# Mamba loop: state on 128 partitions, chosen rows scaled between exponentials, residual update behind masked B and C

## The chip, the cores and the metric

One core of a Trainium2 chip runs the program. The metric is the device time of one execution in microseconds; the median of three runs is compared. The profile comes from one execution of its own.

## What is computed

x is (4, 1024, 256). Three layers run in turn, each behind a plain layer norm: a mixture of 8 experts (top 2, squared ReLU, times 0.5), a Mamba block, and the same mixture again. The Mamba block matters here:

```python
xn = (x - mu) * rsqrt(var + EPS) * ln_w + ln_b
u = xn @ W_in                       # z (512), xBC (544), dt (64)
dt = softplus(u[..., -NHEADS:] + dt_bias)
xBC = silu(causal_conv4(xBC) + conv_b)
xs, Bm, Cm = xBC split in 64 heads x 8, 16, 16
A = -exp(A_log)
def step(h, inp):                   # over 1024 steps, h is (4, 64, 8, 16)
    h = h * exp(dt_t * A) + dt_t x_t B_t
    y = h C_t
g = (y + Dp * xs) * silu(z)
g = g * rsqrt(mean(g * g) + EPS) * rms_w
return x + g @ W_out
```

The outer sum then adds the layer's normed input once more, so the update of x is x + (normed x) + g @ W_out.

## The kernel before

Three stages run one after the other: routing and experts (0 to about 330 us), the Mamba loop (about 376 to 985), routing and experts again. In the Mamba stage 32 chunks k are worked on. A chunk is 32 time steps of all 4 sequences, 128 tokens on 128 partitions. The recurrence is cut up by chunk: inside a chunk the heads' outputs are matrix products with decay factors (`decays`, `intra`); between chunks a state `Hs` is carried.

`Hs` lies on 64 partitions (4 sequences x 16 state entries) and has 512 columns (64 heads x 8). The 0/1 mask `C_HALF` leaves in `bm` and `cm` (64 x 128) for each token only the 16 rows of its own sequence. For chunk k the state takes this way:

- TensorE `sums`, L1199: running sums of dt*A in `banks[0]`, three groups of 64 columns: up to the token, past the token, whole chunk. ScalarE `sums`, L1062, exponentiates all 192 columns into `ee`.
- TensorE `inter`, L1204: `cm` times `Hs` into `banks[7]` (128 x 512). VectorE `carried`, L890, multiplies it by `ee` into `yi`.
- VectorE `weighted`, L896, makes `dtxw`; `skipped`, L903, adds the D term to `yi`; `faded`, L908, multiplies `Hs` by the chunk's decay.
- TensorE `state`, L1224: B transposed (`bt`) times `dtxw` into `banks[7][0:64]`, once `carried` has read the bank; VectorE `state`, L914, adds it to `Hs`.

The other names that count: L920 `decays` (four products of decay factors and B.C pairs, from ScalarE's exponentials L1068 of TensorE's L1217), L856 `conv` (15 operations), L884 `gate_in`, L862 `silu` (needs ScalarE's tanh `tanh_conv`, L1109), L868 and L869 `masked`, L834 to L844 `steps` (dt and dt*A by a chain of small operations), L874 `pairs`, L879 `stepped` (`dtx`), L933 `finish` (the update of x with the row factor `mss` that GpSimd makes in `rms`, L985 and L989, from the sum of squares of ScalarE's `squares`, L1073).

The two rows of expert output that were chosen for each token are loaded by SyncE (`load`), scaled by ScalarE (`choices`, L1056, two operations) and added to x by GpSimd's accumulating DMAs (`add_choice`, L1000, the first of a chunk one round before it is normed).

Nothing schedules this: each engine has one function with a loop over i that calls these steps for chunks i-1 to i+5 in a written order, and it works through them strictly in that order, waiting on semaphores. `after(engine, name, count)` is such a wait, for a buffer to come free. On VectorE a round is `carried`, `weighted`, `skipped`, `faded`, `stats`, `decays` 0, `gate`, `state`, `decays` 1, `norm`, `decays` 2 and 3, `conv`, `finish`, `gate_in`, `silu`, `masked`, `steps`, `pairs`, `stepped`. On ScalarE the round ends with `channels`, `turned_b` (L1146, which waits for VectorE's `pairs`) and `choices`.

Of the kernel before, what the change touches and what calls it, by code (L numbers as in the profile page):

```python
# [14 lines left out]
P = 128  # L15
# [66 lines left out]
def build(nc, a, out):  # L82
    with ExitStack() as ctx:
# [6 lines left out]
        banks = [ctx.enter_context(nc.psum_tensor(f"bank{i}", [P, 512], F32)) for i in range(8)]  # L90
# [106 lines left out]
        cm = [sb(f"cm{p}", [B * DS_, P]) for p in range(2)]  # L197
# [11 lines left out]
        ee = sb("ee", [P, 3 * NH])  # L209
        Hs = sb("Hs", [B * DS_, DI])  # L210
# [577 lines left out]
        sums_ps = banks[0][:, 2 * P + NH:2 * P + 4 * NH]  # L788
# [6 lines left out]
        def mamba_dve(dve):  # L795
# [69 lines left out]
            def masked(k):  # L865
                n = B * DS_
                dve.wait_ge(S("m_si"), k + 1)
                dve.tensor_tensor(bm[:, :], th[0:n, NB * P:], const(C_HALF)[0:n, :], ALU.mult).then_inc(S("m_g"), 1)  # L868
                dve.tensor_tensor(cm[k % 2][:, :], th[n:2 * n, NB * P:], const(C_HALF)[n:2 * n, :], ALU.mult)\  # L869
                    .then_inc(S("m_g"), 1)  # L870
# [65 lines left out]
            for i in range(FIRST, LAST):  # L936
# [110 lines left out]
        def mamba_act(act):  # L1047
# [94 lines left out]

            def turned_b(k):
                act.wait_ge(S("m_cbp"), k + 1)
                act.wait_ge(S("m_cb"), k + 1)
                act.activation(bt[k % 2][:, :], bt_ps, ACT.Copy).then_inc(S("m_bt"), 1)  # L1146

            for i in range(FIRST, LAST):
                if inside(i):
                    sums(i)  # L1150
                    decays(i, 0)
                    decays(i, 1)
                    decays(i, 2)
                    decays(i, 3)
# [17 lines left out]
                if inside(i + 1):  # L1172
                    turned_b(i + 1)
                if inside(i + 4):
                    choices(i + 4)

        def mamba_pe(pe):
# [13 lines left out]
            def sums(k):  # L1191
# [5 lines left out]
                for i, mask in enumerate((upto16, past16, chunk16)):  # L1197
# [22 lines left out]
            def state(k):  # L1220
# [3 lines left out]
                pe.matmul(banks[7][0:B * DS_, :], bt[k % 2][:, :], dtxw[:, :], start=True, stop=True).then_inc(S("m_sp"), 1)  # L1224
# [70 lines left out]
            def pairs(k):  # L1295
# [6 lines left out]
                for b in range(B):  # L1302
                    pe.matmul(cb_ps, bm[:, :], cm[k % 2][:, b * QT:(b + 1) * QT], start=b == 0, stop=b == B - 1)
# [149 lines left out]
```

## Time and profile before

| | us |
|---|---|
| three runs | 1360.13, 1356.54, 1357.54, median 1357.54 |
| profiled execution, time | 1360.11 |
| its span in the trace | 1358.3 |
| Mamba loop, 376.0 to 985.5 | 609.5 |
| VectorE busy in it | 537.8 |
| TensorE busy in it | 525.1 |
| ScalarE busy in it | 327.9 |
| GpSimd busy in it | 279.4 |

The span leaves out 1.8 us that the execution's time has. Busy time of VectorE and ScalarE counts operations alone, which overlap a little at their ends, so 128x512 elements take 0.68 us but the next operation starts 0.60 behind. Spans on GpSimd are rough.

### The profile page before, as it was taken

Reading aid. Unit: us, or ns where it says so; the run is one execution under the profiler, and the core shown is the slowest. Engines: PE = TensorE matmul, PEld = TensorE weight load, DVE = VectorE, ACT = ScalarE, POOL = GpSimd, SP = SyncE. Lnnn points to the kernel's source line nnn. Section 1 sums busy time; section 2 is a strip of 40 time slices with the busy share of each in tenths; the row PEclk is TensorE's granted clock in tenths of the full one; section 3 lists DMA queues with packets and bytes.
Section 4 is the critical chain, followed back from the end, with each engine's and each line's share of the span. In section 5 each row is a group of like instructions: output and inputs, shape, how many; then the busy total and the mean of one; then the engine's idle time right before and its main releaser. Section 6 shows DMA issues by size and latency. Waiting matters only on the chain.

```text
span 1358.3 us, 39743 instructions
## 1 busy us (share of the span) xinstructions
PE 1037.0 (76%) x14336; PEld 864.3 (64%) x14336; DVE 1000.1 (74%) x3102; ACT 635.2 (47%) x1458; POOL 591.1 (44%) x497
## 2 busy tenths in 40 slices
PE   3551999997488898888888888888856419999970
PEld 3441899986465676666666656666645419999960
DVE  4984666665488889888888888889847636666648
ACT  2331566554355555555555555555422205656540
POOL 2785233334234455354445544543217762333330
PEclk9999999999599989998999999999865559999995
DMA  9546444443233333333333333332202244444449
GB/s 232 176 169 189 89 103 96 103 97 102 66 62 73 75 62 63 75 70 62 72 76 68 62 72 71 66 64 56 48 17 79 91 121 92 100 100 103 97 102 344
DMA packets 180704, 131.22 MB, mean 97 GB/s; under 512 B 112417, under 2 KB 152353, under 8 KB 180385
## 3 DMA queue, kind: packets, MB, share of 16 engines
q1 hardware_dynamic: 147488, 69.72, 21.3%
q0 software_dynamic: 27264, 53.71, 16.6%
q10 hardware_dynamic: 5760, 5.26, 1.2%
q8 instruction: 119, 1.95, 0.6%
q14 instruction: 73, 0.59, 0.2%
HBM read 41.34 MB, written 51.61 MB: 68 GB/s over the span
## 4 chain that ended last, share of the span: by engine, by line
PE 27%; DVE 22%; POOL 19%; issue 13%; SPq 8%; DMA 7%; ACT 3%; POOLq 0%; DVEq 0%; ACTq 0%
PE bank L648 10%; PE bank L662 10%; POOL disp L547 7%; POOL mss L989 5%; SPq L598 4%; POOL mss L985 4%; DVE q_ L836 4%; DVE cv L856 2%; DMA arena<-disp 2%; DVE th L862 2%; SPq L600 2%; PE bank L1224 2%; PE bank L1217 1%; DMA disp<-arena,sloti 1%; DVE gz L884 1%
## 5 line engine op out<-in xcount | busy, mean ns | idle before, releaser
L648 PE MATMUL bank<-arena,weights 128*128 128x128 f16 x3456 | 221.1, 222 | 59.6 <-DMA arena<-disp 59.2
L607 POOL DMA_INDIRECT ychosen<-arena,didx x144 | 141.8, 985 | 270.9 <-DVE didx L713 243.1
L648 PEld LDWEIGHTS bank<-arena,weights 128*128 x3456 | 207.8, 99 | 66.8 <-issue 63.2
L721 DVE TENSOR_TENSOR arena<-arena 128x512 f32<-128x512 f32 x144 | 99.7, 693 | 156.2 <-ACT arena L683 155.3
L662 PE MATMUL bank<-weights,arena 128*128 x1728 | 211.5, 273 | 0.0
L683 ACT ACTIVATE arena<-bank 128x512 f32<-128x512 f32 x144 | 86.0, 597 | 192.0 <-PE bank L648 183.5
L662 PEld LDWEIGHTS bank<-weights,arena 128*128 128x128 f16 x1728 | 163.2, 98 | 16.4
L547 POOL DMA_INDIRECT disp<-arena,sloti x128 | 134.9, 1054 | 59.4 <-issue 35.5
L856 DVE SCALAR_TENSOR_TENSOR cv<-U,vec,cv 128x128 f32<-128x128 f32 x480 | 128.5, 339 | 0.0
L1217 PEld LDWEIGHTS bank<-a,arena 128*128 128x128 f16 x2048 | 71.7, 103 | 65.3 <-issue 55.1
L1068 ACT ACTIVATE arena<-bank 128x512 f32<-128x512 f32 x128 | 70.7, 597 | 84.8 <-PE bank L1217 84.6
L989 POOL TENSOR_TENSOR mss<-mss,mhalf 128x1 f32<-128x1 f32 x32 | 107.0, 3345 | 5.9 <-POOL mss L985 5.9
L1000 POOL DMA_DIRECT2D X<-yg x64 | 55.1, 861 | 121.9 <-ACT yg L1056 112.1
L726 DVE TENSOR_TENSOR arena<-arena 128x512 f16<-128x512 f32 x144 | 99.6, 692 | 5.3 <-DVE arena L721 0.4
L687 ACT ACTIVATE arena<-arena 128x512 f16<-128x512 f32 x144 | 90.7, 630 | 4.6
L489 PE MATMUL bank<-cst,arena 128*128 128x128 f32 x128 | 31.4, 427 | 75.9 <-DVE arena L319 70.7
L1217 PE MATMUL bank<-a,arena 128*128 128x64 f16 x2048 | 82.0, 201 | 3.8 <-DVE dtx L879 3.6
L920 DVE TENSOR_TENSOR arena<-arena,cb 128x512 f32<-128x512 f32 x128 | 84.2, 678 | 0.3 <-issue 0.2
L985 POOL TENSOR_SCALAR mss<-mss 128x1 f32<-128x1 f32 x32 | 69.1, 2160 | 34.4 <-ACT tz L1073 34.1
L1243 PE MATMUL bank<-wo,arena 128*128 128x256 f32 x256 | 65.6, 400 | 22.0 <-ACT arena L1078 22.0
L995 POOL DMA_DIRECT2D yi<-turned_y x32 | 29.0, 905 | 112.9 <-DMA turned_y<-y 109.9
L489 PEld LDWEIGHTS bank<-cst,arena 128*128 128x128 f32 x128 | 25.5, 226 | 77.7 <-DVE arena L319 59.5
(157 smaller groups left out, 2104.8 us busy)
## 6 DMA issues: line engine op xcount, KB each, us to landing
arena<-in_w SPq DMA_DIRECT2D x16, 512.0 KB, 4.7
yg<-ychosen SPq DMA_DIRECT2D x32, 256.0 KB, 2.8
X<-yg POOLq DMA_DIRECT2D x64, 128.0 KB, 2.9
arena<-dtx SPq DMA_DIRECT2D x128, 64.0 KB, 2.8
turned_y<-y SPq DMA_DIRECT2D x128, 64.0 KB, 1.8
yi<-turned_y POOLq DMA_DIRECT2D x32, 256.0 KB, 4.1
arena<-ychosen SPq DMA_DIRECT2D x32, 256.0 KB, 5.5
X<-in_x SPq DMA_DIRECT2D x32, 128.0 KB, 4.5
```

What stands on the lines that cost most here:

```text
L547: pool.indirect_dma_start(disp, bass.IndirectOffsetOnAxis(ap=sloti[p][:, 2 * j + x:2 * j + x + 1], axis=0), drow[p][:, j * ROW:(j + 1) * R ...
L607: pool.indirect_dma_start(ychosen, bass.IndirectOffsetOnAxis(ap=didx[:, t % NIDX:t % NIDX + 1], axis=0), ysb[t % YB][:, :], None).then_inc ...
L648: mm = pe.matmul(o, chunk(where, 2 * ("hl".index(w) * WN + c * HID + m * P), P), v, start=c == 0 and n_ == 0, stop=c == KD - 1 and n_ == 2)
L662: mm = pe.matmul(o, x, chunk(where, 2 * ((2 + "hl".index(w)) * WN + c * D), D), start=c == 0 and n_ == 0, stop=c == KH - 1 and n_ == 2)
L683: act.activation(hr[t % 2][:, :], banks[2 + t % 2][:, :], ACT.Relu, scale=1.0 / WSCALE).then_inc(S("hr"), 1)
L687: act.activation(hh[t % HB][:, :], hr[t % 2][:, :], ACT.Square).then_inc(S("hh"), 1)
L721: dve.tensor_tensor(hq[t % 2][:, :], hr[t % 2][:, :], hr[t % 2][:, :], ALU.mult).then_inc(S("hq"), 1)
L726: dve.tensor_tensor(hl[t % HB][:, :], hq[t % 2][:, :], hh[t % HB][:, :], ALU.subtract).then_inc(S("hl"), 1)
L856: dve.scalar_tensor_tensor(out=o, in0=taps(p, c, QT)[:, j], scalar=vc(V_CW, j * DC + c, 1), in1=o, op0=ALU.mult, op1=ALU.add).then_inc(S(" ...
L985: pool.tensor_scalar(mss[:, 1:2], mss[:, 0:1], 1.0 / DI, 4.0 * EPS, ALU.mult, ALU.add)\
L989: pool.tensor_tensor(mss[:, 2:3], mss[:, 1:2], mhalf[:, 0:1], ALU.pow).then_inc(S("m_rr"), 1)
L1217: m = pe.matmul(o, upto[:, t * P:(t + 1) * P], a16[p][:, n * NH:(n + 1) * NH], start=n == 0, stop=n == 1)
```

## The change

- `Hs` becomes 128 x 256: partitions 0 to 63 hold the first 32 heads, 64 to 127 the others. `faded` and `state` on VectorE work on 128 x 256 in place of 64 x 512. The whole-chunk sums in `banks[0]` are made for the half of the heads that a partition holds (four matmuls of 32 columns in place of two of 64), and `ee` has 160 columns.
- `inter` and `state` on TensorE become two matmuls each, of 256 columns: `inter` contracts over 64 partitions for each half, into `across`, which is the last 256 columns of `banks[6]` and the first 256 of `banks[7]`; `state` writes 64 partitions of `banks[7]` for each half.
- `cm` needs C on both halves: ScalarE copies it (`spread_c`, new, ahead of `turned_b`), and `inter` waits for it (`m_cm`). Since `across` reaches into `banks[6]`, `inter` also waits for `y1` of the chunk before, and `intra` for `carried`.
- ScalarE's `choices(i+4)` moves from the end of round i to behind the first two exponentials of round i.
- VectorE's `finish(i-1)` moves from behind `conv` to behind `masked`.

```diff
+        across = two_banks[:, 256:768]
-        cm = [sb(f"cm{p}", [B * DS_, P]) for p in range(2)]
+        cm = [sb(f"cm{p}", [2 * B * DS_, P]) for p in range(2)]
-        ee = sb("ee", [P, 3 * NH])
-        Hs = sb("Hs", [B * DS_, DI])
+        ee = sb("ee", [P, 2 * NH + NH // 2])
+        Hs = sb("Hs", [2 * B * DS_, DI // 2])
...
             def faded(k):
                 dve.wait_ge(S("m_inter"), k + 1)
                 dve.wait_ge(S("m_ee"), k + 1)
-                dve.tensor_tensor(by_head(Hs[:, :]), by_head(Hs[:, :]), heads(ee[0:B * DS_, 2 * NH:], HP), ALU.mult)\
+                by_half = Hs[:, :].rearrange("p (h e) -> p h e", e=HP)
+                dve.tensor_tensor(by_half, by_half, ee[:, 2 * NH:].unsqueeze(2).to_broadcast([P, NH // 2, HP]), ALU.mult)\
...
-                dve.tensor_tensor(Hs[:, :], Hs[:, :], banks[7][0:B * DS_, :], ALU.add).then_inc(S("m_state"), 1)
+                dve.tensor_tensor(Hs[:, :], Hs[:, :], banks[7][:, 0:DI // 2], ALU.add).then_inc(S("m_state"), 1)
...
+            def spread_c(k):
+                act.wait_ge(S("m_g"), 2 * (k + 1))
+                after(act, "m_inter", k - 1)
+                n = B * DS_
+                act.activation(cm[k % 2][n:2 * n, :], cm[k % 2][0:n, :], ACT.Copy).then_inc(S("m_cm"), 1)
...
             def inter(k):
                 pe.wait_ge(S("m_state"), k + 1)
-                pe.matmul(banks[7][:, :], cm[k % 2][:, :], Hs[:, :], start=True, stop=True).then_inc(S("m_inter"), 1)
+                pe.wait_ge(S("m_cm"), k + 1)
+                after(pe, "m_y1", k)
+                for r in range(2):
+                    rows = slice(r * B * DS_, (r + 1) * B * DS_)
+                    m = pe.matmul(across[:, r * DI // 2:(r + 1) * DI // 2], cm[k % 2][rows, :], Hs[rows, :], start=True, stop=True)
+                m.then_inc(S("m_inter"), 1)
...
-                pe.matmul(banks[7][0:B * DS_, :], bt[k % 2][:, :], dtxw[:, :], start=True, stop=True).then_inc(S("m_sp"), 1)
+                for r in range(2):
+                    m = pe.matmul(banks[7][r * B * DS_:(r + 1) * B * DS_, 0:DI // 2], bt[k % 2][:, :],
+                                  dtxw[:, r * DI // 2:(r + 1) * DI // 2], start=True, stop=True)
+                m.then_inc(S("m_sp"), 1)
...
             def intra(k):
                 pe.wait_ge(S("m_bd"), 16 * B * (k + 1))
                 after(pe, "m_y1", k)
+                pe.wait_ge(S("m_yi"), k + 1)
```

VectorE from the convolution to the small chain, in a round in the middle of the loop, before:

```order
662 L856 SCALAR_TENSOR_TENSOR cv<-U,vec,cv 128x128 x15
663 L933 SCALAR_TENSOR_TENSOR X<-bank,mss,X 128x256
664 L884 SCALAR_TENSOR_TENSOR gz<-tz,bank 128x512
665 L862 SCALAR_TENSOR_TENSOR th<-th,cv 128x640
666 L868 TENSOR_TENSOR bm<-th,cst 64x128
667 L869 TENSOR_TENSOR cm<-th,cst 64x128
668 L834 TENSOR_SCALAR q_<-e_ 128x64
```

and the same place of the changed kernel:

```order
662 L859 SCALAR_TENSOR_TENSOR cv<-U,vec,cv 128x128 x15
663 L887 SCALAR_TENSOR_TENSOR gz<-tz,bank 128x512
664 L865 SCALAR_TENSOR_TENSOR th<-th,cv 128x640
665 L871 TENSOR_TENSOR bm<-th,cst 64x128
666 L872 TENSOR_TENSOR cm<-th,cst 64x128
667 L937 SCALAR_TENSOR_TENSOR X<-bank,mss,X 128x256
668 L837 TENSOR_SCALAR q_<-e_ 128x64
```

The update of x stands four operations later; the small chain begins at the same position.

ScalarE from the last channel operation to behind the exponentials, before (yg is the pair of chosen rows, arena the decay factors):

```order
388 L1140 ACTIVATE U<-bank 128x16x32
389 L1146 ACTIVATE bt<-bank 128x64
390 L1056 ACTIVATE yg<-yg,wts 128x256 x2
391 L1062 ACTIVATE ee<-bank 128x192
392 L1068 ACTIVATE arena<-bank 128x64x8 x4
393 L1073 ACTIVATE tz,mss<-G 128x512
```

and after:

```order
419 L1144 ACTIVATE U<-bank 128x16x32
420 L1151 ACTIVATE cm<-cm 64x128
421 L1156 ACTIVATE bt<-bank 128x64
422 L1066 ACTIVATE ee<-bank 128x160
423 L1072 ACTIVATE arena<-bank 128x64x8 x2
424 L1060 ACTIVATE yg<-yg,wts 128x256 x2
425 L1072 ACTIVATE arena<-bank 128x64x8 x2
426 L1077 ACTIVATE tz,mss<-G 128x512
```

Between `bt` and `ee` nothing stands any more, the scalings are between the second and the third exponential, and the copy of C is new ahead of `bt`.

TensorE from the sums to the state's update, before:

```order
526 L1199 MATMUL bank<-a,cst 128x64 x6
527 L1204 MATMUL bank<-Hs,cm 128x512
528 L1217 MATMUL bank<-a,arena 128x64 x32
529 L1224 MATMUL bank<-dtxw,bt 64x512
530 L1217 MATMUL bank<-a,arena 128x64 x32
```

and after:

```order
529 L1213 MATMUL bank<-a,cst 64x32 x4
530 L1216 MATMUL bank<-a,cst 128x64 x4
531 L1225 MATMUL bank<-Hs,cm 128x256 x2
532 L1239 MATMUL bank<-a,arena 128x64 x32
533 L1247 MATMUL bank<-dtxw,bt 64x256 x2
534 L1239 MATMUL bank<-a,arena 128x64 x32
```

The order is the same; the two products with the state are in halves, and the sums have two matmuls more.

## Rows read from the trace of the kernel before

**Rows 1.** The 27 rounds: busy PE, PEld, DVE, ACT, POOL; clock, DMA share, GB/s

```profile
394.17:925.94 531.77, 459.05 (x7209) 341.94 (x7209) 469.34 (x1432) 290.68 (x757) 256.82 (x163) 0.96 0.34 68
```

**Rows 2.** Groups by line, 400 to 980: busy, mean ns, idle before, releaser

```profile
L1068 ACT ACTIVATE arena<-bank 128x512 f32<-128x512 f32 x116 | 64.1, 597 | 75.8 <-PE bank L1217 75.6
...
L890 DVE TENSOR_TENSOR yi<-bank,ee 128x512 f32<-128x512 f32 x29 | 20.1, 692 | 24.0 <-ACT ee L1062 21.2 <-PE bank L1204 2.7
...
L908 DVE TENSOR_TENSOR Hs<-Hs,ee 64x512 f32<-64x512 f32 x29 | 19.6, 677 | 0.0
...
L933 DVE SCALAR_TENSOR_TENSOR X<-bank,mss,X 128x256 f32<-128x256 f32 x30 | 14.5, 484 | 19.5 <-issue 19.5
...
L825 DVE TENSOR_SCALAR xn<-X,ma 128x256 f32<-128x256 f32 x29 | 11.6, 400 | 0.0
```

**Rows 3.** VectorE, one round in order of time: start us, us

```profile
571.74 0.69 DVE L890 TENSOR_TENSOR yi<-bank,ee 128x512 f32<-128x512 f32 x1 [0.84 <-ACT ee L1062]
...
579.11 4.01 DVE L856 SCALAR_TENSOR_TENSOR cv<-U,vec,cv 128x128 f32<-128x128 f32 x15
...
584.64 0.82 DVE L862 SCALAR_TENSOR_TENSOR th<-th,cv 128x640 f32<-128x640 f32 x1
...
589.65 0.68 DVE L879 TENSOR_TENSOR dtx<-bank,dt 128x512 f32<-128x512 f32 x1
591.17 0.69 DVE L890 TENSOR_TENSOR yi<-bank,ee 128x512 f32<-128x512 f32 x1 [0.83 <-ACT ee L1062]
```

**Rows 4.** ScalarE in the same round

```profile
583.16 0.74 ACT L1109 ACTIVATE th<-cv 128x640 f32<-128x640 f32 x1 [0.89 <-DVE cv L856]
...
589.83 0.22 ACT L1146 ACTIVATE bt<-bank 128x64 f32<-128x64 f32 x1 [2.84 <-DVE cb L874]
589.95 0.90 ACT L1056 ACTIVATE yg<-yg,wts 128x256 f32<-128x256 f32 x2
590.75 0.32 ACT L1062 ACTIVATE ee<-bank 128x192 f32<-128x192 f32 x1
```

**Rows 5.** GpSimd's root of the mean square in two rounds

```profile
558.37 5.01 POOL L985 TENSOR_SCALAR mss<-mss 128x1 f32<-128x1 f32 x1 [1.04 <-ACT tz L1073]
563.56 0.56 POOL L989 TENSOR_TENSOR mss<-mss,mhalf 128x1 f32<-128x1 f32 x1 [0.18 <-POOL mss L985]
...
577.76 5.79 POOL L989 TENSOR_TENSOR mss<-mss,mhalf 128x1 f32<-128x1 f32 x1 [0.18 <-POOL mss L985]
```

**Rows 6.** TensorE in the round of rows 3

```profile
573.13 1.04 PE L1224 MATMUL bank<-dtxw,bt 128*64 128x512 f32 x2 [1.52 <-DVE yi L890]
...
585.51 0.66 PE L1292 MATMUL bank<-cst,th 128*128 128x128 f32 x4 [0.56 <-DVE th L862]
...
588.50 1.12 PE L1204 MATMUL bank<-Hs,cm 64*128 64x512 f32 x2
```

**Rows 7.** A round with the low clock: window of 612 to 614, TensorE, ScalarE

```profile
612.00:614.00 2.00, 2.00 (x5) 0.39 (x6) 1.82 (x7) 0.00 (x0) 0.00 (x0) 0.50 0.67 133
...
612.00 1.94 PE L1224 MATMUL bank<-dtxw,bt 128*64 128x512 f32 x2 [1.53 <-DVE yi L890]
...
627.91 1.12 PE L1204 MATMUL bank<-Hs,cm 64*128 64x512 f32 x2
...
622.40 0.73 ACT L1109 ACTIVATE th<-cv 128x640 f32<-128x640 f32 x1
```

**Rows 8.** VectorE in the first round; VectorE and TensorE without rows to scale

```profile
387.63 0.83 DVE L862 SCALAR_TENSOR_TENSOR th<-th,cv 128x640 f32<-128x640 f32 x1 [0.20 <-ACT th L1109]
...
943.92 0.68 DVE L879 TENSOR_TENSOR dtx<-bank,dt 128x512 f32<-128x512 f32 x1
944.64 0.69 DVE L890 TENSOR_TENSOR yi<-bank,ee 128x512 f32<-128x512 f32 x1
...
946.04 1.04 PE L1224 MATMUL bank<-dtxw,bt 128*64 128x512 f32 x2 [0.74 <-DVE yi L890]
```

**Rows 9.** VectorE waiting for TensorE, 670.55 us

```profile
670.55 0.69 DVE L890 TENSOR_TENSOR yi<-bank,ee 128x512 f32<-128x512 f32 x1 [1.53 <-PE bank L1204]
```

More of the change, by code:

```diff
@@ L88, in sem @@
             return ctx.enter_context(nc.semaphore(name))
-        banks = [ctx.enter_context(nc.psum_tensor(f"bank{i}", [P, 512], F32)) for i in range(8)]
+        banks = [ctx.enter_context(nc.psum_tensor(f"bank{i}", [P, 512], F32)) for i in range(6)]
+        two_banks = ctx.enter_context(nc.psum_tensor("bank67", [P, 1024], F32))
+        banks += [two_banks[:, 0:512], two_banks[:, 512:1024]]
+        across = two_banks[:, 256:768]
         weights = sb("weights", [P, 4 * 2 * WN], U8)
@@ L787, in build @@
         v_ps = banks[0][:, 2 * P:2 * P + NH]
-        sums_ps = banks[0][:, 2 * P + NH:2 * P + 4 * NH]
+        sums_ps = banks[0][:, 2 * P + NH:2 * P + 3 * NH + NH // 2]
         cb_ps, bt_ps = banks[2][:, P:P + QT], banks[2][:, P + QT:P + QT + B * DS_]
@@ L957, in mamba_dve @@
                     conv(i + 1)
-                if inside(i - 1):
-                    finish(i - 1)
                 if inside(i):
@@ L964, in mamba_dve @@
                     masked(i + 1)
+                if inside(i - 1):
+                    finish(i - 1)
                 if inside(i + 2):
@@ L1152, in mamba_act @@
                     decays(i, 1)
+                if inside(i + 4):
+                    choices(i + 4)
+                if inside(i):
                     decays(i, 2)
@@ L1172, in mamba_act @@
                 if inside(i + 1):
+                    spread_c(i + 1)
                     turned_b(i + 1)
-                if inside(i + 4):
-                    choices(i + 4)
         def mamba_pe(pe):
@@ L1196, in sums @@
                     pe.wait_ge(S("m_v"), k + 2)
-                for i, mask in enumerate((upto16, past16, chunk16)):
+                for r in range(2):
+                    rows = slice(r * B * DS_, (r + 1) * B * DS_)
+                    for n in range(2):
+                        part = a16[p][:, n * NH + r * NH // 2:n * NH + (r + 1) * NH // 2]
+                        pe.matmul(sums_ps[rows, 2 * NH:], chunk16[:, rows], part, start=n == 0, stop=n == 1)
+                for i, mask in enumerate((upto16, past16)):
                     for n in range(2):
@@ L1203, in inter @@
                 pe.wait_ge(S("m_state"), k + 1)
-                pe.matmul(banks[7][:, :], cm[k % 2][:, :], Hs[:, :], start=True, stop=True).then_inc(S("m_inter"), 1)
+                pe.wait_ge(S("m_cm"), k + 1)
+                after(pe, "m_y1", k)
+                for r in range(2):
+                    rows = slice(r * B * DS_, (r + 1) * B * DS_)
+                    m = pe.matmul(across[:, r * DI // 2:(r + 1) * DI // 2], cm[k % 2][rows, :], Hs[rows, :], start=True, stop=True)
+                m.then_inc(S("m_inter"), 1)
             def decays(k, g):
@@ L1223, in state @@
                 pe.wait_ge(S("m_bt"), k + 1)
-                pe.matmul(banks[7][0:B * DS_, :], bt[k % 2][:, :], dtxw[:, :], start=True, stop=True).then_inc(S("m_sp"), 1)
+                for r in range(2):
+                    m = pe.matmul(banks[7][r * B * DS_:(r + 1) * B * DS_, 0:DI // 2], bt[k % 2][:, :],
+                                  dtxw[:, r * DI // 2:(r + 1) * DI // 2], start=True, stop=True)
+                m.then_inc(S("m_sp"), 1)
             def gate_in(k):
@@ L1302, in pairs @@
                 for b in range(B):
-                    pe.matmul(cb_ps, bm[:, :], cm[k % 2][:, b * QT:(b + 1) * QT], start=b == 0, stop=b == B - 1)
+                    pe.matmul(cb_ps, bm[:, :], cm[k % 2][0:n, b * QT:(b + 1) * QT], start=b == 0, stop=b == B - 1)
                 pe.transpose(bt_ps, bm[:, :], ident[0:n, 0:n]).then_inc(S("m_cbp"), 1)
```

4 lines of the change are left out of this document (2 added, 2 removed).

## The prediction

> **What bounds the kernel now.** I read the windows first: the Mamba loop is the only stage that the diff touches, and in 531.77 us of it VectorE is busy for 469.34, TensorE for 459.05 at a mean clock of 0.96 of full [rows 1]. Then the groups by line inside the loop, for VectorE's idle time: it waits in only two places, 24.0 us before L890 (the state's contribution `yi`, released by ScalarE's `ee`) and 19.5 us before L933 (`finish`) [rows 2]. Then the timeline of one round, from one L890 to the next. 27 rounds lie between 394.17 and 925.94, 531.77 us, 19.70 us each [rows 1]. A plain round takes 19.43 us (571.74 to 591.17) [rows 3]: VectorE works through with its two gaps. So VectorE's own order sets the round, and a microsecond cut from it counts 27 to 32 times, as long as TensorE stays behind it.
>
> TensorE's path I count from its first L1224 of a round, called S here. S stands 1.39 us after L890 starts (571.74 to 573.13) [rows 3, 6]. The next L1204 ends at 589.62, S+16.49, of which 0.56 is TensorE's wait for VectorE's `th` [rows 6]. Without that wait TensorE would need 15.93 + 0.07 + 1.39 = 17.39 us for a round. That is the floor under everything below.
>
> **Moving `choices` behind two exponentials.** ScalarE's `bt` copy starts 589.83, then the two row scalings (0.90 us), then `ee` at 590.75, which ends 591.07; L890 starts 591.17 although `dtx` (started 589.65, 0.68 long) ended 590.33 [rows 3, 4]. Without the scalings `ee` follows `bt` 0.12 us on (the step from 589.83 to 589.95), 0.80 earlier. The trace holds the edited state already: the last rounds have no rows to scale, and there L890 follows the start of `dtx` by 0.72 us (943.92 to 944.64), with no idle noted [rows 8], against 1.52 us (589.65 to 591.17) [rows 3]. Gain 0.80 per round, for the 26 or so rounds whose wait ends at `ee`. What the scalings land on: ScalarE idles 75.6 us before 116 exponentials for TensorE's L1217 [rows 2], which is 2.6 a round, the most of it behind the first two, so 0.90 us is covered; if that cover went, it would cost at most the 0.90 once more. Their input is loaded a round before. GpSimd's first add of chosen rows comes earlier, into idle time, and it is queued ahead of `ma` L980, which waits for VectorE anyway.
>
> **State on 128 partitions.** L908 (677 ns) and L914, both 64x512, go to 128x256 [rows 2]. The nearest rows of 128x256 are L825 at 400 ns and L933 at 484 ns, from PSUM and with a scalar [rows 2], so each saves 0.19 to 0.28 us; I take 0.25, since one source is SBUF as at L825. 0.50 per round, 16 us over 32 rounds if VectorE bounds all of them (12 to 18 by the two ends). `ee` shrinks by 32 columns, worth a few hundredths. The copy of C to the upper partitions goes ahead of `bt`, where ScalarE idles 2.84 us [rows 4]; it takes about the 0.22 us of `bt`. TensorE must have it before L1204; ScalarE is done with its channels at 586.99 (589.83 less 2.84), 1.5 us before L1204's 588.50, so nothing waits.
>
> On TensorE L1204 and L1224 become two matmuls each of half the columns: at the same rate per column they stay at 1.12 and 1.04 us [rows 6]. Nothing in the trace runs two row halves side by side, so the ends are minus 0.5 us each (side by side) and plus 0.35 each (two more weight loads that nothing hides). I take 0, plus 0.1 for the two more mask matmuls: TensorE's floor is 17.5.
> A rule on this stands in the Trainium skill, "TensorEngine Tiling (Array Packing)", Key Properties: different tiles can load weights and multiply in parallel, but changing the tiling mode drains the engine. By its first half the floor would fall below 17; the VectorE sum would be the same.
>
> **Moving `finish` behind `masked`.** Now L933 waits 0.5 to 0.9 us and is 0.48 long, of which the next operation overlaps 0.08; the convolution ends at 583.12 and `th` L862 starts 584.64, 1.52 us behind it [rows 2, 3]. Ahead of L862 only the gate's product (0.60) remains, but it also needs ScalarE's tanh, which starts at 583.16 and takes 0.74 [rows 4]. The first round, which has no `finish`, shows what is left: 0.20 us idle before L862 [rows 8], so 0.81 behind the convolution. Gain 0.71, less the 0.40 that `finish` takes later: 0.31. Where L933 waited 0.9 instead of 0.5 the gain is larger if tanh is on time.
>
> **Sum for a plain round.** 19.43 - 0.80 - 0.50 - 0.31 = 17.82, above TensorE's 17.5: VectorE still bounds, barely. 14 of the 27 rounds are plain: 14 x 1.61 = 22.5 us.
>
> **Rounds with the low clock.** In 10 of the 27 rounds (S = 434.43 to 887.69) the first L1224 pair takes 1.6 to 1.9 us instead of 1.04; at 612 to 614 us the granted clock is 0.50, the 1.2 GHz level, after 1.53 us in which TensorE waited for VectorE's `yi` and `dtxw` [rows 6, 7]. There everything behind it is late: tanh starts at 622.40, S+10.40 [rows 7], because the copy of `y` is ahead of it. In the changed order L862 then starts at S+11.2; from L862 to `dtx` 5.01 (584.64 to 589.65), plus `finish` 0.40, plus 0.72 to L890, plus 1.39 to S: 18.7 instead of 19.80. (TensorE alone: L1204 ends 629.03, S+17.03, which with 0.07 and 1.39 gives 18.5.) 10 x 1.0 = 10 us. The other 3 rounds hold TensorE's stalls; L890 at 670.55 waited 1.53 us for L1204 [rows 9], and nothing of the change shortens that: 1 us together.
> With the round before the 27 (0.8 + 0.5), the rounds behind them (0.8 each) and the tail, 3.5 us: 22.5 + 10 + 1 + 3.5 = 37 us.
> TensorE's wait before S shrinks by the 0.80. In the rounds without scalings it is 0.74 already, and the pair there takes 1.04 us [rows 8]; that is little to go by. If half of the 10 low rounds stay at full clock, that gives another 5 x 0.9 = 4.5; I take 3. Together **40 us**. The profiled execution took 1360.1 us (span 1358.3 and 1.8 around it), so it would be 1320.1; it stands 2.6 above the median 1357.5, so the forecast is **1317.5, say 1318 us**.
>
> **Rivals.**
> (a) GpSimd misses its gap. L985 and L989 take 0.28 to 0.56 us alone, but 5.01 and 5.79 when they meet the convolution, and both are released at its end (563.38, 583.55) [rows 5]. So they get through only while VectorE does not read two SBUF operands. Behind the convolution the gate's product (one operand in PSUM) and the wait for tanh leave 0.81 us; L989 ends 0.43 behind it in a plain round (583.55 against 583.12); where L985 itself was held to 563.38, L989 ended at 564.12, 0.74 later. If it misses, it is shut out through L862 and `masked`, and `finish` waits about 0.5 us behind them: 6 us for the late kind alone, 15 for all: 1324 to 1333. Chance 0.12.
> The rule is in the Trainium skill, "SBUF — State Buffer", Who interferes with whom: the port pair of VectorE and GpSimd is an exclusive lock, and an operation with two SBUF inputs contends with GpSimd's reads. The 5.01 against 0.28 us agrees.
> (b) TensorE or ScalarE becomes the bound. The unhidden weight loads (+0.7) put TensorE at 18.2, and in the low rounds at 19.3; 14 x 1.2, 10 x 0.5 and 4.5 leave 26 us: 1331. For it: TensorE is within 0.4 us already. Against: half of its waits are for VectorE. Chance 0.10.
> (c) More than forecast: halves side by side, low rounds gone. 24 rounds at 17.8 and 3 with stalls at 19.4 give 46 us, the ends 3.5: 1308, or 1305 if the stalls shrink too. Chance 0.12.
> (d) Slower. VectorE no longer waits, so TensorE's clock decides: one low stretch costs TensorE 1.1 us (S+17.03 against S+15.93). From the second in every round (17.5 + 2.2 = 19.7) the gain is gone; three give 20.8, 27 x 1.1 = 30 us over: 1387. For it: only that the stretches fall where nothing in the order puts them. Against: TensorE will idle less than now, and one in three rounds has one. Chance 0.03.
> (e) It does not do what it says: the next thing queued on ScalarE holds `ee` again, as `bt` waits for VectorE's `cb`. Then only 0.8 a round is left: 1335; with (b) and (a), down to no change. Against it stands the 0.72 of the rounds without scalings [rows 8]. Chance 0.05, 0.03 of it for no change.
>
> **How the numbers follow.** Forecast 1318 (1311 to 1324) has 0.58. Taking in (c) in part and (a) gives 1308 to 1333 for 8 in 10. About 0.3% (4 us) is what a measurement can tell from no change: faster by more 0.94, within 0.03, slower 0.03.
>
> **What would show it.** No idle over 0.1 us before L890's successor; about 0.2 us before L862's, more in rounds with late `y`; none before `finish`; `Hs` operations near 0.40 and 0.45 us; rounds of 17.8; first L1224 pair low in fewer than 10. It is wrong if rounds stand at 18.3 or more with TensorE never waiting for `yi`, or if an idle gap is released by GpSimd's `mss` or by the copy of C.

## The result, and the profile after

The changed kernel takes 1302.43 us (median of four runs, 1300.31 to 1302.90) against 1358.84 us (four runs of before, 1356.54 to 1361.51): a ratio of 0.9581, 95% interval 0.9559 to 0.9604. That is 56 us less. The forecast was 40 us less, 1318, and 1308 to 1333 for 8 in 10: the direction and the plain rounds were right, the size was not, and the time lies 5.6 us below that range.

The profiled execution took 1302.08 us, its span is 1300.3. Over the 27 rounds that answer to [rows 1] (columns as there):

```profile
391.69:875.49 483.80, 424.08 (x7371) 336.78 (x7371) 455.03 (x1431) 302.50 (x784) 147.23 (x162) 1.00 0.39 75
```

483.80 us in place of 531.77, 17.92 a round. VectorE is busy for 94% of it (before 88%), TensorE's mean granted clock is 1.00 in place of 0.96, and GpSimd's busy time fell from 256.82 to 147.23 us, which the forecast did not have.

The groups by line from 380 to 920 us (busy, mean ns, idle before and its releaser), for [rows 2]:

```profile
L865 DVE SCALAR_TENSOR_TENSOR th<-th,cv 128x640 f32<-128x640 f32 x30 | 24.8, 825 | 7.5 <-ACT th L1113 7.5
...
L893 DVE TENSOR_TENSOR yi<-bank,ee 128x512 f32<-128x512 f32 x30 | 20.8, 692 | 2.1 <-PE bank L1225 1.2 <-issue 0.4
...
L937 DVE SCALAR_TENSOR_TENSOR X<-bank,mss,X 128x256 f32<-128x256 f32 x29 | 14.0, 484 | 0.9
L912 DVE TENSOR_TENSOR Hs<-Hs,ee 128x256 f32<-128x256 f32 x30 | 12.6, 420 | 0.0
L918 DVE TENSOR_TENSOR Hs<-Hs,bank 128x256 f32<-128x256 f32 x30 | 12.4, 415 | 0.0
```

The idle time ahead of L893 fell from 24.0 to 2.1 us, that ahead of `finish` from 19.5 to 0.9; new is 7.5 us ahead of `th` L865. The state's two operations take 0.42 us in place of 0.68. One round on VectorE and the same place on ScalarE, for [rows 3, 4]:

```profile
462.82 0.69 DVE L893 TENSOR_TENSOR yi<-bank,ee 128x512 f32<-128x512 f32 x1
...
469.85 4.02 DVE L859 SCALAR_TENSOR_TENSOR cv<-U,vec,cv 128x128 f32<-128x128 f32 x15
...
474.67 0.83 DVE L865 SCALAR_TENSOR_TENSOR th<-th,cv 128x640 f32<-128x640 f32 x1 [0.21 <-ACT th L1113]
...
476.17 0.48 DVE L937 SCALAR_TENSOR_TENSOR X<-bank,mss,X 128x256 f32<-128x256 f32 x1
...
480.79 0.69 DVE L893 TENSOR_TENSOR yi<-bank,ee 128x512 f32<-128x512 f32 x1
```

```profile
462.30 0.22 ACT L1156 ACTIVATE bt<-bank 128x64 f32<-128x64 f32 x1 [1.83 <-DVE cb L877]
462.42 0.30 ACT L1066 ACTIVATE ee<-bank 128x160 f32<-128x160 f32 x1
...
464.03 0.90 ACT L1060 ACTIVATE yg<-yg,wts 128x256 f32<-128x256 f32 x2
```

`ee` follows `bt` 0.12 us on, as forecast; the scalings stand where ScalarE waits. `th` starts 0.80 us behind the convolution's end (473.87), with 0.21 us of waiting: 0.81 and 0.20 were forecast. This round takes 17.97 us, with a stall in it; the plain ones (409.47 to 427.25, 427.25 to 445.04 and 17 more of the 27) take 17.77 to 17.79. Forecast: 17.82. TensorE in the same round, for [rows 6]:

```profile
462.86 0.64 PE L1239 MATMUL bank<-a,arena 128*128 128x64 f16 x16 [0.55 <-DVE dtx L882]
464.21 0.65 PE L1247 MATMUL bank<-dtxw,bt 128*64 128x256 f32 x4 [0.71 <-DVE yi L893]
...
478.77 0.70 PE L1225 MATMUL bank<-Hs,cm 64*128 64x256 f32 x4
```

The halves run side by side: 0.65 and 0.70 us for four instructions, against 1.04 and 1.12 for two of twice the columns. The wait ahead of the state's matmul is 0.71 us in place of 1.53, and in none of the rounds is that group slower than 0.65. Of the rounds with the low clock one is left, 731.26 to 750.70:

```profile
731.26:750.70 19.44, 16.92 (x261) 13.73 (x262) 16.84 (x53) 11.11 (x29) 5.48 (x6) 0.91 0.28 55
...
741.75 0.25 PE L1310 MATMUL bank<-arena 128*32 128x32 f32 x3 [1.07 <-issue]
```

Its clock falls at 743.4 us, behind a stall of TensorE of 1.07 us at another place than the wait for `yi`. And GpSimd, for [rows 5]:

```profile
468.31 0.34 POOL L989 TENSOR_SCALAR mss<-mss 128x1 f32<-128x1 f32 x1
468.83 1.52 POOL L993 TENSOR_TENSOR mss<-mss,mhalf 128x1 f32<-128x1 f32 x1 [0.18 <-POOL mss L989]
```

The power is done at 470.35, 0.5 us into the convolution, and so it is in every round that has a convolution. Before, either it was held for 5.79 us or the operation ahead of it for some 5 us [rows 5], and it ended 0.4 to 0.8 us behind the convolution.

Three questions follow. Are the three gains of a round what the forecast says, one by one? What took away the low clock? Why does the convolution no longer shut GpSimd out, and what is that worth?

### The profile page after: what moved, and what is told of

Read it like the earlier page. It is cut to its first block, busy times and chain, and to the rows that moved or that the text cites. A ratio compares the mean times of both kernels' runs of the same rounds, so it can differ in the third digit from the quotient of the medians.

```text
span 1300.3 us, 40252 instructions
## 1 busy us (share of the span) xinstructions
PE 996.0 (77%) x14528; PEld 859.2 (66%) x14528; DVE 985.8 (76%) x3102; ACT 647.9 (50%) x1490; POOL 469.8 (36%) x497
## 4 chain that ended last, share of the span: by engine, by line
DVE 35%; PE 18%; SPq 17%; issue 13%; POOL 8%; DMA 6%; ACT 3%; DVEq 0%; POOLq 0%; ACTq 0%
SPq L601 9%; DVE cv L859 8%; POOL disp L550 7%; PE bank L665 6%; PE bank L651 6%; DVE q_ L839 4%; DVE arena L924 4%; SPq L603 4%; DVE th L865 2%; PE bank L1199 2%; ACT th L1113 2%; SPq L584 2%; DVE yi L906 1%; DVE G L931 1%; DMA disp<-arena,sloti 1%
## 5 line engine op out<-in xcount | busy, mean ns | idle before, releaser
L1239 PEld LDWEIGHTS bank<-a,arena 128*128 128x128 f16 x2048 | 64.9, 98 | 46.4 <-DVE dtx L882 23.2
L984 POOL TENSOR_TENSOR ma<-ma,mhalf 128x2 f32<-128x2 f32 x32 | 30.9, 966 | 167.4 <-DVE ma L823 167.4
L1239 PE MATMUL bank<-a,arena 128*128 128x64 f16 x2048 | 75.8, 193 | 19.9 <-DVE dtx L882 19.8
L1004 POOL DMA_DIRECT2D X<-yg x64 | 64.0, 1001 | 18.6 <-DMA X<-yg 11.6
L1268 PEld LDWEIGHTS bank<-wo,arena 128*128 128x128 f32 x256 | 47.1, 194 | 35.1 <-ACT arena L1082 29.8
```

Source lines behind the costliest of these rows:

```text
L1239: m = pe.matmul(o, upto[:, t * P:(t + 1) * P], a16[p][:, n * NH:(n + 1) * NH], start=n == 0, stop=n == 1)
L1268: m = pe.matmul(banks[5][:, 0:D], GT[:, j * P:(j + 1) * P], wo[:, j * D:(j + 1) * D], start=j == 0, stop=j == NB - 1)
```

## The experiments

Each kernel is compared with the kernel before on the same chip. Three chips served; the kernel before takes 1356.5 us on the first, 1365.8 and 1366.5 on the others. Theory A: TensorE's long wait for VectorE ahead of the state's matmul lets the clock fall. Theory B: it is something else, and the rounds with the low clock stay.

The expectations speak of a slow first pair of that matmul. A fall that comes a little later leaves the pair at full speed and slows the matmuls behind it, so the count below goes by the granted clock: stretches of the 27 rounds in which it stands near 0.50, the lower of the two levels. A stretch "behind the wait" begins within about 1 us of the start of the state's matmul, every other one more than 10 us later.

| kernel | wait ahead of the state's matmul, us | low stretches behind the wait | others |
|---|---|---|---|
| before | 1.53 | 9 | 2 |
| finish alone | 1.53 or 1.41 | 10 | 0 |
| state on 128 partitions alone | 1.50 or 1.20 | 10 | 0 |
| changed, choices back | 1.50 | 11 | 1 |
| choices alone | 0.74 | 0 | 1 |
| before, TensorE kept busy | 0.59 | 0 | 2 |
| changed | 0.71 | 0 | 1 |
| changed, finish back | 0.71 | 0 | 0 |

**Choices alone, on the kernel before.**

```diff
                     decays(i, 0)
                     decays(i, 1)
+                if inside(i + 4):
+                    choices(i + 4)
...
                     turned_b(i + 1)
-                if inside(i + 4):
-                    choices(i + 4)
```

> The kernel before with one edit: ScalarE's choices stand between the second and third exponential. Both theories: L890 no longer waits 0.84 us, a plain round goes from 19.44 to 18.64. Theory A (TensorE's one long wait ahead of the state's matmul, 1.53 us, is what lets its clock fall): the wait shrinks to 0.74, no round has a slow first pair (1.6 to 1.9 us instead of 1.04), all in all 24 to 25 us less than before. Theory B (low rounds come from something else and stay at about 10 of 27): 21 us less, at most.

Measured: ratio 0.9810 (0.9763 to 0.9856), 27 us less; the 27 rounds of the profile take 506.61 us against 531.77, 25.2 less. Plain rounds 18.63 to 18.64, to the hundredth as expected. No low stretch is left behind the wait; the one that remains begins 16 us into a round. Theory A holds here.

**Finish alone, on the kernel before.**

```diff
-                if inside(i - 1):
-                    finish(i - 1)
                 if inside(i):
                     gate_in(i)
                 if inside(i + 1):
                     silu(i + 1)
                     masked(i + 1)
+                if inside(i - 1):
+                    finish(i - 1)
```

> The kernel before with one edit: VectorE's finish behind masked. A plain round goes from 19.44 to 19.13, since L862 comes 0.71 earlier and finish costs 0.40 later; rounds with the low clock from 19.80 to 19.5. TensorE's wait of 1.53 us stays, so both theories keep low rounds, about 10 of 27. 9 us less than before. If GpSimd misses its gap, finish waits 0.5 us and nothing is gained.

Measured: 0.9954 (0.9930 to 0.9978), 5.5 us less by the medians, 9.1 in the 27 rounds. Plain rounds 19.12, ten low stretches. `finish` never waited in them; GpSimd's power still took 3.9 us on average, and ended 0.4 to 0.8 us behind the convolution, which is early enough for the new place. Rival (a) of the prediction is out.

**State on 128 partitions alone.** The edit is against the changed kernel: `finish` and `choices` go back to their old places.

```diff
+                if inside(i - 1):
+                    finish(i - 1)
                 if inside(i):
                     gate_in(i)
...
                     silu(i + 1)
                     masked(i + 1)
-                if inside(i - 1):
-                    finish(i - 1)
...
                     decays(i, 0)
                     decays(i, 1)
-                if inside(i + 4):
-                    choices(i + 4)
-                if inside(i):
                     decays(i, 2)
...
                     spread_c(i + 1)
                     turned_b(i + 1)
+                if inside(i + 4):
+                    choices(i + 4)
```

> The changed kernel with choices and finish back in their old places: only the state on 128 partitions. VectorE's two operations save 0.26 each, so a plain round goes from 19.44 to 18.93, 16 us less than before. TensorE's two products take 0.7 instead of 1.1 us, so it waits longer for VectorE, 1.5 us ahead of the state's matmul as before and more ahead of that. Theory A: low rounds stay, 10 of 27 or more. A rival, that they went because TensorE's own path became 0.8 us shorter: none is left.

Measured: 0.9721 (0.9679 to 0.9763), 38 us less where 16 were expected; 29.8 of them lie in the 27 rounds. Plain rounds take 18.28 and not 18.93. VectorE and GpSimd in one of them:

```profile
395.75 4.03 DVE L859 SCALAR_TENSOR_TENSOR cv<-U,vec,cv 128x128 f32<-128x128 f32 x15
399.69 0.48 DVE L937 SCALAR_TENSOR_TENSOR X<-bank,mss,X 128x256 f32<-128x256 f32 x1
400.09 0.68 DVE L887 SCALAR_TENSOR_TENSOR gz<-tz,bank 128x512 f32<-128x512 f32 x1
400.68 0.82 DVE L865 SCALAR_TENSOR_TENSOR th<-th,cv 128x640 f32<-128x640 f32 x1
```

```profile
394.74 1.53 POOL L993 TENSOR_TENSOR mss<-mss,mhalf 128x1 f32<-128x1 f32 x1 [0.18 <-POOL mss L989]
```

`finish` starts with the end of the convolution, without the 0.52 us of before. So this part brings 0.54 us by shorter operations and 0.6 us by a wait that disappears. Ten low stretches are left, as Theory A expected, each behind a wait of 1.50 us or more and none behind one of 1.2. Only in three of these rounds is the first group of the state's matmul clearly slow; in most the fall comes just behind it, and the round still takes 18.9 to 19.0 us:

```profile
408.59 0.65 PE L1246 MATMUL bank<-dtxw,bt 128*64 128x256 f32 x4 [1.50 <-DVE yi L893]
409.17 1.89 PE L1238 MATMUL bank<-a,arena 128*128 128x64 f16 x32
410.87 2.80 PE L1198 MATMUL bank<-wz,xnT 128*128 128x512 f32 x4
```

```profile
409.20:412.20 3.00, 3.00 (x36) 2.48 (x35) 2.82 (x9) 1.70 (x4) 1.68 (x2) 0.50 0.20 48
```

**TensorE kept busy in the wait, kernel before.**

```diff
+FILL = 32
...
             def state(k):
+                after(pe, "m_y1", k)
+                for t in range(FILL):
+                    pe.matmul(banks[6][:, 0:NH], upto16, a16[k % 2][:, 0:NH], start=True, stop=True)
                 pe.wait_ge(S("m_yi"), k + 1)
```

> The kernel before with 32 matmuls of 128x64 fp16 more on TensorE in each round, just ahead of its wait for yi and dtxw; they write into a bank that is free there and that intra overwrites. They take 1.0 of the 1.53 us that TensorE waits. Theory A: no low rounds, the 10 of 27 rounds at 19.80 become 19.44, 3 to 4 us less than before. Theory B: low rounds stay, no change. If the fillers get in the way of the state's matmul, each round gets longer by their excess over 1.5 us.

Measured: 0.9980 (0.9952 to 1.0007), 3.0 us less by the medians; over the 27 rounds of the profile 527.52 us against 531.77. TensorE (the filler is L1224 here, the state's matmul L1228):

```profile
450.34 1.10 PE L1224 MATMUL bank<-a,cst 128*128 128x64 f16 x32
452.03 1.04 PE L1228 MATMUL bank<-dtxw,bt 128*64 128x512 f32 x2 [0.59 <-issue]
```

No low stretch is left behind the wait, where the kernel before has nine, in a kernel whose VectorE does what it did. Work without any use in that one wait keeps the clock up. Two other stretches remain; they begin 16 us into a round. The clock's effect is shown in the rows; the 3 us of the whole kernel are not told from no change by the interval.

**The changed kernel with choices back.**

```diff
                     decays(i, 1)
-                if inside(i + 4):
-                    choices(i + 4)
...
                     turned_b(i + 1)
+                if inside(i + 4):
+                    choices(i + 4)
```

> The changed kernel with choices back at the end of ScalarE's round. L893 waits 0.80 us again, a plain round goes from 17.78 to 18.6: 22 us more than the changed kernel, 1325. TensorE's wait ahead of the state's matmul is 1.5 us again. Theory A (that wait lets the clock fall): low first pairs come back, in some 10 of the rounds, and cost up to 0.9 us each, 1325 to 1334. Theory B: none, 1325.

Measured: 0.9823 (0.9796 to 0.9849), 24 us less than before on that chip; the 27 rounds take 512.23 us, 28 more than the changed kernel's, within the 22 to 31 that Theory A gave. Plain rounds 18.57, and eleven low stretches behind the wait, most of them in rounds of 19.1 to 19.3. Two of its state's matmuls, and the window of the first:

```profile
430.12 1.12 PE L1246 MATMUL bank<-dtxw,bt 128*64 128x256 f32 x4 [1.50 <-DVE yi L893]
449.39 0.65 PE L1246 MATMUL bank<-dtxw,bt 128*64 128x256 f32 x4 [1.50 <-DVE yi L893]
```

```profile
430.10:431.00 0.90, 0.88 (x4) 0.31 (x4) 0.90 (x3) 0.00 (x0) 0.00 (x0) 0.53 1.05 163
```

The granted clock is 0.53 there, the 1.2 GHz level for nearly all of it. With the wait of 1.50 us the low stretches are back: 9, 10, 10 and 11 behind waits of 1.5 us, none behind waits of 0.7 us or with TensorE kept busy. Theory A stands for these. Some of the waits of 1.50 us drop the clock and others, like the second row, don't: which ones stays open. So does what lets it fall elsewhere in a round, once or twice in the 27 rounds of five of the kernels.

It also shows something else: the halves with finish moved (18.57) are slower a round than the halves alone (18.28).

**Why GpSimd gets through.** Two kernels test whether it is the place of GpSimd's operands in memory, which the smaller `Hs` and `ee` had shifted. The first is the one with the state on 128 partitions alone, and a pad; the second is the kernel before with two tensors moved.

```diff
+        pad = sb("pad", [P, 288])
         ma = sb("ma", [P, 6 + 2 + 2 + 2 + 2])
```

> The kernel with the state on 128 partitions alone (choices and finish in their old places), with 1152 bytes of unused memory ahead of ma and mss, so that GpSimd's operands lie where they lay before. In the version without the pad GpSimd's power ran 1.5 us and was done 0.5 us into the convolution, while before it took 5.8 us and ended 0.4 us behind the convolution, and VectorE's finish no longer waited. Theory address (where mss lies decides whether the convolution shuts GpSimd out): 5.8 us again and finish waits 0.5 us. Theory partitions (64-partition operations of VectorE are the cause): 1.5 us, no wait.

```diff
-        ee = sb("ee", [P, 3 * NH])
-        Hs = sb("Hs", [B * DS_, DI])
...
         mss = sb("mss", [P, 3])
+        ee = sb("ee", [P, 3 * NH])
+        Hs = sb("Hs", [B * DS_, DI])
```

> The kernel before with ee and Hs at the end of the memory, so that everything behind them, ma and mss too, lies 2816 bytes lower. Nothing else changes. Theory address: GpSimd's power may run in 1.5 us, finish does not wait, 15 to 19 us less. Theory partitions: 5.8 us, finish waits, the time of before.

Measured, one run each on a chip where the kernel before takes 1365.8: 1331.4 with the pad, the power 1.52 us, `finish` without a wait, 27 rounds in 502.12 us against 502.01 without the pad. 1361.7 with the tensors moved, the power 5.8 us, `finish` waiting 17.0 us in 27 rounds. The address is not the cause.

The third gives VectorE more partitions and no less time:

```diff
-        Hs = sb("Hs", [B * DS_, DI])
+        Hs = sb("Hs", [P, DI])
...
-                dve.tensor_tensor(by_head(Hs[:, :]), by_head(Hs[:, :]), heads(ee[0:B * DS_, 2 * NH:], HP), ALU.mult)\
+                dve.tensor_tensor(by_head(Hs[:, :]), by_head(Hs[:, :]), heads(ee[:, 2 * NH:], HP), ALU.mult)\
...
-                dve.tensor_tensor(Hs[:, :], Hs[:, :], banks[7][0:B * DS_, :], ALU.add).then_inc(S("m_state"), 1)
+                dve.tensor_tensor(Hs[:, :], Hs[:, :], banks[7][:, :], ALU.add).then_inc(S("m_state"), 1)
...
-                pe.matmul(banks[7][:, :], cm[k % 2][:, :], Hs[:, :], start=True, stop=True).then_inc(S("m_inter"), 1)
+                pe.matmul(banks[7][:, :], cm[k % 2][:, :], Hs[0:B * DS_, :], start=True, stop=True).then_inc(S("m_inter"), 1)
```

> The kernel before with Hs on 128 partitions x 512 columns: VectorE's two operations on it work on all partitions (the upper 64 hold numbers that nothing reads) and take 0.68 us as before; TensorE reads the lower 64 as before. Theory partitions: GpSimd's power in 1.5 us, finish does not wait, about 19 us less than before although VectorE does no less work. Theory address (mss lies where it lay): the time of before.

Measured: 1344.6, one run, 21 us less than before on that chip. The two operations still take 0.68 us. `finish` waits in none of the 27 rounds, the plain round is 18.83. Of one round, VectorE and GpSimd:

```profile
455.74 0.68 DVE L914 TENSOR_TENSOR Hs<-Hs,bank 128x512 f32<-128x512 f32 x1
...
457.40 1.28 DVE L920 TENSOR_TENSOR arena<-arena,cb 128x512 f32<-128x512 f32 x2
458.60 4.02 DVE L856 SCALAR_TENSOR_TENSOR cv<-U,vec,cv 128x128 f32<-128x128 f32 x15
462.54 0.47 DVE L933 SCALAR_TENSOR_TENSOR X<-bank,mss,X 128x256 f32<-128x256 f32 x1
```

```profile
457.26 0.56 POOL L989 TENSOR_TENSOR mss<-mss,mhalf 128x1 f32<-128x1 f32 x1 [0.18 <-POOL mss L985]
```

The power starts 1.34 us ahead of the convolution, exactly as in the plain rounds of before (577.76 against 579.11 in [rows 3, 5]), and takes 0.56 us where it took 5.79. The convolution's instructions are the same. Where the power came later, it ran for 0.72 us from 0.3 to 1.0 us into the convolution. The last one asks which of the two operations it is: only L914, the later one, gets 128 partitions.

```diff
-        Hs = sb("Hs", [B * DS_, DI])
+        Hs = sb("Hs", [P, DI])
...
-                dve.tensor_tensor(by_head(Hs[:, :]), by_head(Hs[:, :]), heads(ee[0:B * DS_, 2 * NH:], HP), ALU.mult)\
+                dve.tensor_tensor(by_head(Hs[0:B * DS_, :]), by_head(Hs[0:B * DS_, :]), heads(ee[0:B * DS_, 2 * NH:], HP), ALU.mult)\
...
-                dve.tensor_tensor(Hs[:, :], Hs[:, :], banks[7][0:B * DS_, :], ALU.add).then_inc(S("m_state"), 1)
+                dve.tensor_tensor(Hs[:, :], Hs[:, :], banks[7][:, :], ALU.add).then_inc(S("m_state"), 1)
```

> The kernel before with Hs on 128 partitions x 512 columns, where only the addition L914 works on all 128 partitions and the multiplication L908 on 64 as before (the upper 64 hold numbers that nothing reads). With both on 128 partitions GpSimd's power took 0.56 us and finish did not wait. Theory: the last 64-partition operation ahead of the convolution, L914, decides, so the same here, some 20 us less than before. Rival: L908 or both decide, and the power takes 5.8 us.

Measured: 1355.7 against 1366.5, one run; plain rounds 18.83, `finish` waits in none of the 27 rounds:

```profile
458.32 0.56 POOL L989 TENSOR_TENSOR mss<-mss,mhalf 128x1 f32<-128x1 f32 x1 [0.18 <-POOL mss L985]
```

So widening L914 alone is enough in these rounds. (The 27 rounds take 516.46 us against 514.76 above, with twelve low stretches against seven; that the whole time fell by 11 us and not by 20 lies in the main outside of them.)

It is not a rule on L914 by itself. In the last round that has a convolution no `norm` stands between the decay products, and there it comes out the other way round. GpSimd's two operations in the kernel before, L914 on 64 partitions, convolution at 969.28:

```profile
968.21 0.60 POOL L985 TENSOR_SCALAR mss<-mss 128x1 f32<-128x1 f32 x1 [8.31 <-ACT tz L1073]
969.00 0.79 POOL L989 TENSOR_TENSOR mss<-mss,mhalf 128x1 f32<-128x1 f32 x1 [0.18 <-POOL mss L985]
```

and the first of them in the last kernel, L914 on 128, convolution at 955.99, at the same distance from it:

```profile
954.92 5.14 POOL L985 TENSOR_SCALAR mss<-mss 128x1 f32<-128x1 f32 x1 [7.44 <-ACT tz L1073]
```

So the order of the operations around it counts too, and the mechanism is not shown.

**Better than the changed kernel.** If GpSimd is free anyway, `finish` need not be moved.

> The changed kernel itself, as the standard for the two beside it on the same chip: 0.958 of before, plain rounds of 17.78 us.

> The changed kernel with finish back behind the convolution. On the kernel before, finish waited there for GpSimd; with the state on 128 partitions GpSimd is done in time and finish fills the wait for ScalarE's tanh. Theory (the three gains overlap: moving finish costs 0.29 us a round once GpSimd is free): plain rounds of 17.49, 8 us less than the changed kernel. Rival (finish waits again in the tighter round): the time of the changed kernel or more.

The edit of the second is that of "finish alone" above, undone in the changed kernel. Measured: the changed kernel 0.9578 (0.9549 to 0.9607), 1306.9 us; with finish back 0.9533 (0.9504 to 0.9561), 1302.4 us, 4.4 less by the medians, with intervals that overlap. The rounds settle it: 17.49 in place of 17.78, 475.32 us for 27 against 484.00, 8.7 less as expected; the stages ahead of the loop, which the edit leaves as they are, ended 5.4 us later in this profile (first L893 at 375.08 against 369.64). `finish` fills the wait for tanh:

```profile
433.68 4.02 DVE L859 SCALAR_TENSOR_TENSOR cv<-U,vec,cv 128x128 f32<-128x128 f32 x15
437.63 0.47 DVE L937 SCALAR_TENSOR_TENSOR X<-bank,mss,X 128x256 f32<-128x256 f32 x1
438.02 0.67 DVE L887 SCALAR_TENSOR_TENSOR gz<-tz,bank 128x512 f32<-128x512 f32 x1
438.62 0.81 DVE L865 SCALAR_TENSOR_TENSOR th<-th,cv 128x640 f32<-128x640 f32 x1
```

The convolution can shut GpSimd out here too. In two of the 27 rounds the power started 1.08 and 1.35 us into it, took 3.37 and 3.10 us, and `finish` waited 0.52 us: the rival of the expectation, in two rounds.

```profile
752.04 3.10 POOL L993 TENSOR_TENSOR mss<-mss,mhalf 128x1 f32<-128x1 f32 x1 [0.18 <-POOL mss L989]
755.24 0.49 DVE L937 SCALAR_TENSOR_TENSOR X<-bank,mss,X 128x256 f32<-128x256 f32 x1 [0.52 <-issue]
```

The next step keeps `finish` behind the convolution and puts the masked products between links of the small chain.

```diff
-                cb_.link(dve.tensor_scalar(q_[:, :], e_[:, :], LOG1P[-1], None, ALU.mult))
+                cb_.link(dve.tensor_scalar(q_[:, :], e_[:, :], LOG1P[-1], None, ALU.mult), between)
...
+                if inside(i + 1):
+                    between += [lambda: masked_b(i + 1), lambda: masked_c(i + 1)]
```

> As b1_no_finish, and VectorE's two masked products stand between the first links of the chain of small operations that makes dt. A link starts 0.26 us behind the one before, of which the engine works about 0.13; two links are hidden behind the products: 0.2 to 0.3 us less a round, plain rounds of 17.2 to 17.3, 6 to 8 us less than b1_no_finish. If TensorE, which waits for the products, becomes the bound, nothing is gained.

Measured: 0.9491 (0.9457 to 0.9524), 1294.2 us, 8.3 less than with finish back; plain rounds 17.13. VectorE:

```profile
437.97 0.19 DVE L840 TENSOR_SCALAR q_<-e_ 128x64 f32<-128x64 f32 x1
438.09 0.28 DVE L876 TENSOR_TENSOR bm<-th,cst 64x128 f32<-64x128 f32 x1
438.30 0.21 DVE L842 SCALAR_TENSOR_TENSOR q_<-q_,e_ 128x64 f32<-128x64 f32 x1
438.54 0.29 DVE L880 TENSOR_TENSOR cm<-th,cst 64x128 f32<-64x128 f32 x1
```

This is the fastest kernel of the study, 12.7 us below the changed one on the same chip.

## Why the prediction was right in its rounds and short in its sum

**Choices: right.** 0.80 a round forecast, 0.80 measured alone (19.44 to 18.64) and 0.79 on top of the others (18.57 to 17.78). The rounds without scalings in the trace of before had shown it.

**Shorter state operations: right in size.** 0.25 each forecast, 0.26 measured (677 to 420 ns, 0.67 us to 415 ns).

**Finish: right on the kernel before** (0.31 forecast, 19.44 to 19.12 measured), **and wrong as a part of this change.** The forecast took GpSimd's lateness as given: "they get through only while VectorE does not read two SBUF operands". With the state on 128 partitions GpSimd is on time and `finish` would not wait in its old place either. The two edits remove the same wait: alone they give 1.16 and 0.32, together 0.87 (19.44 to 18.57). The plain round came out right, 17.78 for 17.82, in part by luck: the forecast counted that wait once, without knowing that the state's edit also removes it; but the move, which the forecast credits with 0.31, costs 0.29 in the changed kernel.

The port rule that I had named, of the Trainium skill, "SBUF — State Buffer", Who interferes with whom, says that a VectorE operation with two SBUF inputs contends with GpSimd's reads. In the changed kernel the trace agrees for the decay products in front of the convolution: the power, started among them, takes 1.52 us. The convolution has two SBUF inputs as well. In the kernels with L914 on 128 partitions the power is through 0.5 or 1.0 us into it, and is held to its end where it starts 1.08 us into it or later; with L914 on 64 partitions it is held through all of it, the last round excepted. The rule does not tell these apart, and the forecast's "only while VectorE does not read two SBUF operands" was too strong. The measurement decides.

**Rounds with the low clock: the term that was mis-sized.** This is the largest part of the miss. The ten rounds with a slow first pair took 198.6 us before; the forecast took off 10 us and 3 more for those that might go, to 185.6. At 17.78 each they would be 177.8: 7.8 us more than forecast. All of the stretches behind the wait went. The mechanism had been named (TensorE's wait shrinks by 0.80, and the rounds with 0.74 were not low), and I gave it half. The kernels with choices alone and with the filler show that the wait alone is enough. The reading of the rounds was a little off as well: 13 of the 27 and not 14 are plain (nine at 19.43 to 19.44, four at 19.50 to 19.55), and one of the ten slow pairs had no wait ahead of it; its low stretch began at 488.5 us, late in the round before.

**Stalled rounds: left 6.7 us above plain ones, measured 3.7.** The other 17 rounds took 333.2 us before, 2.8 more than plain ones. The forecast took off 22.5 and 1, which leaves 6.7 more than 17 rounds of 17.82, because "nothing of the change shortens that". The changed kernel has 3.7, with the one low stretch in it. That is 3.0 us. With choices alone, where TensorE's matmuls have their old length, it is about 3.4. So the stalls shrink with the rounds also without the halves; what covers them stays open.

**TensorE's halves: taken at 0, measured at minus 0.39 and minus 0.42 us.** A row that showed it was in the trace of before, `intra`:

```profile
580.28 1.30 PE L1284 MATMUL bank<-arena 128*32 128x32 f32 x128
```

These are 128 x 32 = 4096 columns in 1.30 us; at the rate of L1224 (2 x 512 columns in 1.04 us) one behind the other they would take about 4.2, an estimate. So they run side by side. The Trainium skill, "TensorEngine Tiling (Array Packing)", Key Properties, says that different tiles load and multiply in parallel; the 0.65 and 0.70 us agree. It moved no plain round, since VectorE bounds them. Whether it helped the stalled ones is not shown.

With 0.04 us on each plain round (0.7), these make up the 11.5 us by which the 27 rounds gained more than forecast (48.0 for 36.5).

**Outside of the 27 rounds** 10 us were gained where 3.5 were forecast: 1.2 ahead of the first round, 1.3 in it, 2.9 in the last ones, 1.1 behind them, and 3.5 in the second routing and expert stage. The first and the last part are no effect of the change that the traces can show. The loop starts anywhere between 369.6 and 377.0 us in the traces of this study, and at 369.6 and 374.9 in two of the changed kernel. From the last update of x to the end it takes 351.6 us before and 348.1 after, but also 351.6 with choices alone, 351.5 with finish alone and 348.4 in the filler's kernel, whose layout is that of before.

**Rivals.** (a) and (b) did not come: GpSimd did not miss its gap, TensorE waits as long as forecast or longer. (c), more than forecast, is what happened, with both of its conditions, of which the low rounds are shown to count; it gave 1308 or 1305, and the rest lies in the stages outside of the loop. (d) had the clock right as the thing to watch and the sign wrong. (e) did not come either: of the 2.1 us of idle time left ahead of L893, none is put down to `ee`.

## What to carry to other kernels

Where a trace shows some rounds slow by the clock, look at the one wait ahead of the slow matmuls: if the change shortens that wait, count the slow rounds as gone, and give the case its own number. Count them by the granted clock of each round, not by the time of one group: the fall can come just behind it. Two edits that remove the same wait are worth it once, so after each gain undo the others one at a time; here one of three had become a loss. And an operation on half of the partitions can cost another engine more than its own time: here it held GpSimd's power for 5.79 us in place of 0.56, and VectorE waited about 0.6 us a round for that.

## What the runs showed of the hardware that I had not expected

With L914 on 64 partitions GpSimd's power, started 1.34 us ahead of the convolution, was held through two decay products and 15 convolution operations (5.79 us). With L914 on 128 partitions and 512 columns, for the same time on VectorE, it took 0.56 us; the address of the operands had no part in it. In the one round without `norm` it was the other way round (0.79 us behind a 64-partition L914; its forerunner L985 held for 5.14 us behind a 128-partition one). The convolution's operations themselves changed by a few ns with it (median 339 ns before, 337 with the tensors moved, 343 with L914 and L908 on 128 partitions, 347 in the changed kernel), at the same distance of 0.26 us. What in VectorE or in the port keeps GpSimd out stays open; `bm` and `cm`, also on 64 partitions, have no GpSimd operation queued behind them that would tell.

Four matmul instructions of 256 columns in two halves of the rows took 0.70 us, in two halves of the columns 0.65 us, at the full clock; at the low level 1.11 to 1.23 and 1.12.

32 useless matmuls of 64 columns a round, 1.1 us of them, kept TensorE's clock at its high level behind a wait that had dropped it in nine rounds of 27.
